# Row norms in a fused four-layer transformer kernel: the inverse root by one GpSimd power in place of eleven VectorE steps

## The reference, cut to what matters

```python
def _layernorm(x, axis=-1, eps=1e-05):
    m = jnp.mean(x, axis=axis, keepdims=True)
    v = jnp.var(x, axis=axis, keepdims=True)
    return (x - m) / jnp.sqrt(v + eps)

x = x + jnp.tanh(g_xattn[0]) * _L0_xattn_ref(_layernorm(x, axis=-1), ctx_1024, ctx_1024)
x = x + jnp.tanh(g_ffn[0]) * _L0_ffn_ref(_layernorm(x, axis=-1), ...)
x = x + jnp.tanh(g_xattn[1]) * _L1_xattn_ref(_layernorm(x, axis=-1), ctx_1024, ...)
x = x + jnp.tanh(g_ffn[1]) * _L1_ffn_ref(_layernorm(x, axis=-1), ...)
x = x + jnp.tanh(g_xattn[2]) * _L2_xattn_ref(_layernorm(x, axis=-1), ctx_1024, ctx_1024, mask_BxSxS2_bf0, ...)
x = x + jnp.tanh(g_ffn[2]) * _L2_ffn_ref(_layernorm(x, axis=-1), ...)
x = x + jnp.tanh(g_xattn[3]) * _L3_xattn_ref(ctx_1024, _layernorm(x, axis=-1), mask_BxS2_bf1, ...)
x = x + jnp.tanh(g_ffn[3]) * _L3_ffn_ref(_layernorm(x, axis=-1), ...)
```

## Time and profile before

| | |
|---|---|
| median of three runs | 1993.43 us |
| the profiled execution: its own time | 1995.64 us |
| its span, first to last instruction | 1993.9 us |
| PE busy | 1498.6 us, 75% |
| DVE busy | 1258.8 us, 63%, 4319 instructions |
| ACT busy | 782.1 us, 39% |
| POOL busy | 359.6 us, 18%, 242 instructions |
| mean granted clock of PE | 0.854 of full speed |

### The profile page before, as it was taken

One profiled execution on the slowest core, in us unless ns is written; L12 is line 12 of the kernel. 1 busy time (PEld: TensorE's weight loads), 2 busy tenths in 40 slices (PEclk: granted clock), 3 DMA queues, 4 the chain that ended last, 5 costly groups with the idle time before them and its releaser, 6 DMA issues. The chain is left out here.

```text
span 1993.9 us, 29626 instructions
## 1 busy us (share of the span) xinstructions
PE 1498.6 (75%) x10926; PEld 955.8 (48%) x10926; DVE 1258.8 (63%) x4319; ACT 782.1 (39%) x1473; POOL 359.6 (18%) x242
## 2 busy tenths in 40 slices
PE   5779586877688947787868875778786795778777
PEld 4447343553555724354545552346454464335545
DVE  5466875557646786555755688555564659755567
ACT  0335333653133523464314442356322353236522
POOL 0204101420031401240003230123002132014200
PEclk7889778988898968898779996889897897789988
DMA  7000000000000000000000000000000000000000
GB/s 286 1 1 1 0 1 0 1 1 14 7 1 1 1 0 1 1 1 13 2 7 1 1 1 1 1 1 2 14 1 7 1 1 1 1 1 1 1 14 6
DMA packets 16846, 19.80 MB, mean 10 GB/s; under 512 B 3352, under 2 KB 15400, under 8 KB 16172
## 3 DMA queue, kind: packets, MB, share of 16 engines
q1 hardware_dynamic: 16688, 17.75, 2.6%
HBM read 16.70 MB, written 1.05 MB: 9 GB/s over the span
## 5 line engine op out<-in xcount | busy, mean ns | idle before, releaser
L1003 POOL TENSOR_TENSOR work<-work 128x1024 f32<-128x1024 f32 x32 | 76.2, 2383 | 312.8 <-ACT work L987 312.8
L932 PE MATMUL bank<-xnT,w_f 128*128 128x512 f32 x256 | 123.2, 626 | 11.9 <-ACT work L984 11.9
L984 ACT ACTIVATE work<-bank,w_f 128x512 f32<-128x512 f32 x128 | 84.2, 684 | 108.9 <-PE bank L932 107.9
L943 PEld LDWEIGHTS bank<-w_f1d,work 128*128 128x128 f32 x1024 | 116.9, 192 | 7.7 <-ACT work L984 3.8
L943 PE MATMUL bank<-w_f1d,work 128*128 128x129 f32 x1024 | 116.9, 275 | 0.0
L1493 POOL TENSOR_TENSOR small<-small 128x16 f32<-128x16 f32 x28 | 81.3, 2903 | 191.1 <-DVE small L1514 190.9
L1513 DVE TENSOR_REDUCE small<-work 128x16 f32<-128x1024 f32 x48 | 58.3, 1215 | 90.4 <-ACT work L1404 86.4
L462 PE MATMUL bank<-consts,work 128*128 128x128 f32 x384 | 74.3, 331 | 50.0 <-ACT work L514 49.1
L1285 PE MATMUL bank<-consts,work 128*128 128x128 f32 x640 | 87.9, 283 | 27.7 <-ACT work L1413 10.7
L328 ACT COPY xnT<-bank 128x256 f32<-128x256 f32 x56 | 20.5, 373 | 211.0 <-PE bank L322 210.8
L462 PEld LDWEIGHTS bank<-consts,work 128*128 128x128 f32 x384 | 49.5, 165 | 108.9 <-ACT work L514 89.8
(11 more groups left out here) (278 smaller groups left out, 3490.5 us busy)
## 6 DMA issues: line engine op xcount, KB each, us to landing
w_f<-in_f_dram SPq DMA_DIRECT2D x1, 2616.0 KB
w_f<-in_f_dram SPq DMA_DIRECT2D x1, 2180.0 KB, 26.2
w_x<-in_x_dram SPq DMA_DIRECT2D x1, 2115.0 KB
w_l<-in_l_dram SPq DMA_DIRECT2D x1, 2088.5 KB, 21.2
w_f1d<-in_f1d_dram SPq DMA_DIRECT2D x4, 512.0 KB
work<-in_x_dram SPq DMA_DIRECT2D x5, 256.0 KB, 3.0
work<-in_ctx_dram SPq DMA_DIRECT2D x5, 256.0 KB, 3.4
out_dram<-x SPq DMA_DIRECT2D x4, 256.0 KB, 2.3
```

What stands on the lines that cost most here:

```text
L932: pe.matmul(banks[n % 3][:, :], k_f1["w1"][:, e * 512 + c * P:e * 512 + (c + 1) * P], xnT[:, :], start=True, stop=True).then_inc(up_done, 1)
L943: pe.matmul(z_of(e, t)[:, 0:129], hT[e % 2][:, c, t * P:(t + 1) * P], w_f1d[:, c, e, :], start=(c == 0), stop=(c == 3))
L984: act.activation(hT[e % 2][:, c, :], banks[n % 3][:, :], ACT.Relu, bias=k_f1["b1"][:, n:n + 1]).then_inc(hT_ready, 1)
L1003: link(pool.tensor_tensor(sq[e % 2][:, 0:2, :], sq[e % 2][:, 0:2, :], sq[e % 2][:, 2:4, :], ALU.add))
```

## The change

Where `norm_pair` stood behind the attentions of turns 1 and 3 and behind the perceiver, `norm_pair_by_pool` stands now, and `rms_pair`, behind the attention of turn 6, works in the same way: DVE writes variance plus epsilon of the pair's two tiles into a tensor of two columns and raises a semaphore, POOL takes both columns to the power -0.5 by one instruction, and DVE waits for it and goes on to the two scalings. `attention` gets a part for POOL (two such powers), the perceiver's part for POOL gets one behind `root_keys(6)` and one behind `root_keys(7)`. A column pair of -0.5 is set once ahead of the loop. `ffn0`, `ffn1`, `ffn2`, the opening of the next block and the last norm keep the eleven steps. `layer_norm` by POOL has fewer steps (`yield`s), so that `some(next_rows, 7)` in step 4 of `attention` now runs the whole norm of a pair, its wait for POOL and its scalings too. The core of the diff:

```diff
+        def ask_root(dve, ins):
+            ins.then_inc(variance_ready, 1)
+            roots["asked"] += 1
+            return roots["asked"]
+
+        def give_root(pool):
+            roots["given"] += 1
+            pool.wait_ge(variance_ready, roots["given"])
+            pool.tensor_tensor(root[:, :], variance[:, :], minus_half[:, :], ALU.pow).then_inc(root_ready, 1)
...
+            if by_pool:
+                rs = root
+                k = ask_root(dve, dve.tensor_scalar(variance[:, :], mv[:, :, 1], LN_EPS, None, ALU.add))
+                yield
+                dve.wait_ge(root_ready, k)
+            else:
+                link(dve.tensor_scalar(ve, mv[:, :, 1], LN_EPS, None, ALU.add))
+                yield
+                yield from rsqrt(dve, link, rs, ve, tmp)
...
+        def norm_pair_by_pool(dve, link, pair):
+
+            yield from layer_norm(dve, link, [(x, xn, t) for t in pair_tiles(pair)], by_pool=True)
+            dve.sem_inc(rows_ready, 1)
...
+        def rms_pair(dve, link, pair):
+
+            ms = scratch()[:, 0:2]
...
-            link(dve.tensor_scalar(ms, ms, 1.0 / D, RMS_EPS, ALU.mult, ALU.add))
+            k = ask_root(dve, dve.tensor_scalar(variance[:, :], ms, 1.0 / D, RMS_EPS, ALU.mult, ALU.add))
             yield
-            yield from rsqrt(dve, link, rs, ms, tmp)
-            return rs
...
+            dve.wait_ge(root_ready, k)
+            link.last_of([dve.scalar_tensor_tensor(xn[:, t, :], xn[:, t, :], root[:, t % 2:t % 2 + 1], k_f3["n1"],
                                                    ALU.mult, ALU.mult) for t in pair_tiles(pair)])
             dve.sem_inc(rows_ready, 1)
...
+                @block.gpsimd
+                def _(pool):
+                    for pair in range(2):
+                        give_root(pool)
...
+                        if b in (6, n - 1):
+                            give_root(pool)
...
+                pool.memset(minus_half[:, :], -0.5)
```

More of the change, by code:

```diff
@@ L184, in build @@
         small = sb("small", [P, 976])
+        variance = sb("variance", [P, 2])
+        root = sb("root", [P, 2])
+        minus_half = sb("minus_half", [P, 2])
         norm_small = sb("norm_small", [P, 256])
@@ L220, in build @@
         stages = []
-        flow = named("rows_ready rows_turned rowsT_ready dve_steps")
-        rows_ready, rows_turned, rowsT_ready, steps_sem = flow
+        flow = named("rows_ready rows_turned rowsT_ready dve_steps variance_ready root_ready")
+        rows_ready, rows_turned, rowsT_ready, steps_sem, variance_ready, root_ready = flow
         dve_steps = Chain(steps_sem)
@@ L238, in build, with layer_norm @@
         scratch.turn = 0
-        def layer_norm(dve, link, jobs):
+        roots = dict(asked=0, given=0)
+        def ask_root(dve, ins):
[6 more added lines that the diff above has]
+            pool.tensor_tensor(root[:, :], variance[:, :], minus_half[:, :], ALU.pow).then_inc(root_ready, 1)
+        def layer_norm(dve, link, jobs, by_pool=False):
             n, s = len(jobs), scratch()
@@ L249, in layer_norm @@
             yield
-            link(dve.tensor_scalar(ve, mv[:, :, 1], LN_EPS, None, ALU.add))
-            yield
-            yield from rsqrt(dve, link, rs, ve, tmp)
+            if by_pool:
[7 more added lines that the diff above has]
+                yield from rsqrt(dve, link, rs, ve, tmp)
             link.last_of([dve.tensor_scalar(dst[:, t, :], src[:, t, :], mv[:, k, 0:1], rs[:, k:k + 1],
@@ L268, in norm_pair_twice @@
             dve.sem_inc(rows_ready, 1)
-        def rms_scales(dve, link, pair):
-            s = scratch()
-            ms, rs, tmp = s[:, 0:2], s[:, 2:4], s[:, 4:6]
+        def rms_pair(dve, link, pair):
+            ms = scratch()[:, 0:2]
             link.last_of([dve.scalar_tensor_tensor(norm_rows[:, t % 2, :], xn[:, t, :], 1.0, xn[:, t, :], ALU.mult,
@@ L277, in rms_scales @@
             yield
-            link(dve.tensor_scalar(ms, ms, 1.0 / D, RMS_EPS, ALU.mult, ALU.add))
+            k = ask_root(dve, dve.tensor_scalar(variance[:, :], ms, 1.0 / D, RMS_EPS, ALU.mult, ALU.add))
             yield
-            yield from rsqrt(dve, link, rs, ms, tmp)
-            return rs
-        def rms_pair(dve, link, pair):
-            rs = yield from rms_scales(dve, link, pair)
-            link.last_of([dve.scalar_tensor_tensor(xn[:, t, :], xn[:, t, :], rs[:, t % 2:t % 2 + 1], k_f3["n1"],
+            dve.wait_ge(root_ready, k)
+            link.last_of([dve.scalar_tensor_tensor(xn[:, t, :], xn[:, t, :], root[:, t % 2:t % 2 + 1], k_f3["n1"],
                                                    ALU.mult, ALU.mult) for t in pair_tiles(pair)])
@@ L1861, in build @@
             prev = ffn0(i, None, 0, norm_pair)
-            prev = attention(prev, 1, norm_pair, k_x1, kv1, [], scaled[:, 0:1], None,
+            prev = attention(prev, 1, norm_pair_by_pool, k_x1, kv1, [], scaled[:, 0:1], None,
                              add_gated(lambda t: tg[:, 1:2], bo1[:, :]))
             prev = ffn1(prev, 2, norm_all)
-            prev = attention(prev, 3, norm_pair, k_x2, kv2, [(kv2.k_ready, 1), (kv2.v_ready, TILES)], None, neg2,
+            prev = attention(prev, 3, norm_pair_by_pool, k_x2, kv2, [(kv2.k_ready, 1), (kv2.v_ready, TILES)], None, neg2,
                              add_gated(lambda t: any2[:, t:t + 1]))
             prev = ffn2(prev, 4, norm_pair_twice)
-            prev = perceiver(prev, 5, norm_pair)
+            prev = perceiver(prev, 5, norm_pair_by_pool)
             prev = attention(prev, 6, rms_pair, k_a3, kv3, None, scaled[:, 1:2], None, add_to_z)
```

## The result

The change took 24 us off, not 9: the median is 1970.4 us (1961.41 to 1980.6) against 1994.51 us (1988.8 to 2002.07) for the kernel before, timed beside it; the ratio is 0.9876, with a 95% interval of 0.9844 to 0.9908. The profiled execution took 1973.64 us, with a span of 1970.8. The forecast was 1984.4 us and its range began at 1974, so the time lies outside it, on the fast side.

What follows compares the result with a forecast made beforehand. No engine is full; a chain of waits bounds the kernel, with 16.0 us of idle PE at the touched hand-overs. The terms -1.3 - 3.85 - 3.8 = -9 us took the median 1993.43 to 1984.4 us, range 1974 to 1999.

Steps and rivals of the forecast that it cites:

- What bounds the kernel: DVE's and PE's chains race for pair 1's transposes; PE idles 16.0 us at the 16 touched hand-overs.
- The round trip: DVE to POOL and back, a: semaphores 0.2 us plus 0.5 for a two-column power, so a = 0.7 us.
- The rival at a = 0.3: A cheaper power at the touched norms: 14 us gained, 1979.5 us; chance 0.15.
- the turn at 1.35: Round-trip length at which gain turns to loss, two columns taking 1.15 us; with the clock case, chance 0.18.
- The delay d: In the three attentions tile 3's reciprocal (L559) starts later: 0.64 us in turns 1 and 3, 0.44 in turn 6.
- Turns 1 and 3: Eight attention ends where PE's chain holds: 8 x 0.64 of delay less 6.4 us of idle, -1.3 us.
- Perceiver: Four ends without delay, each gaining the smaller of 1.5 us and PE's idle: 3.85 us.
- Turn 6: Four attention ends: 2.8 us gained in the first block, 1.0 in the other three, together -3.8 us.
- The rest at nothing: Everything outside the touched hand-overs, such as POOL's queue, the memset and removed DVE instructions, was counted as zero.
- PE's chain moves by d: In the attentions, projection, fill and both pairs' transposes follow L559 and shift by its delay, 0.64 or 0.44 us.
- The clock rival: Longer idle ahead of L488 flips fills to 1.2 GHz, 2.6 us each: 1993 us; chance 0.18 with a partly fixed power cost.
- The full gain of 1969.5: Nothing covers the gain: the full 1.5 us at all 16 ends, needing an earlier fill; chance 0.05.

Runs made afterwards that it cites:

- The late wait: Kernel after the change, with four or five empty steps between DVE's asking and its wait, so tile 3's reciprocal goes first: 1951.16 us, ratio 0.9757.
- the two families: Kernels before and after the change, each plain and with four or eight chained idle DVE steps per block; shift taken off: 1994.5, 1998.9, 1992.3 against 1970.4, 1966.5, 1971.6 us.
- the fill experiment: Kernel before the change, with two unread 512-column products on PE between the pairs' transposes in turns 2, 4, 6 and 7: 2000.13 us, ratio 1.0024.
- the kernel before with the shifts: Kernel before the change, with four or eight chained DVE steps that change nothing, once a block in ffn0: 2002.13 and 1998.66 us, ratios 1.0038 and 1.0031.
- the shifted pairs: Kernels before and after the change, both with four or both with eight chained idle DVE steps per block: 2002.13 against 1969.65 us, 1998.66 against 1978.04 us.
- the 14 kernels: The kernel before the change, the kernel after it and the twelve other kernels of the follow-up experiments, with ratios to the kernel before from 0.9583 to 1.0088.

## Why the prediction was wrong

**What bounds the kernel: right.** Idle of 16.0 us at the touched hand-overs, of which 0.4 us are left (0.25 and 0.13). The chains raced as described.

**The round trip: nearly right.** Forecast a = 0.7; DVE's idle is 0.81 us, as the power takes 0.70 (forecast 0.5) and the two semaphores 0.11. With 0.70, 1.01 and 2.90 us for 2, 4 and 16 columns, one column costs 0.157 us and 0.38 are fixed. The rule that two columns follow from the additions' fixed 0.16 gave 0.5; a power has more of its own. The rival at a = 0.3 is out, and so is the turn at 1.35. The Trainium skill's advice to keep elementwise work on VectorE (GPSIMD Engine Reference, Engine selection) compares one operation with one operation, and here 0.81 us stand against a chain of eleven, 2.18: no run contradicts the page, but taken for the chain it would have pointed the wrong way.

**The delay d: right as a delay.** The reciprocal starts 0.74 us later, forecast 0.64; PE's idle ahead of tile 3's projection is 2.66 us in the second block's turn 1, where it was 1.94, and 2.42 against 1.88 in turn 6. (In the first and third block's turn 1 it is 1.84 and 1.82, as PE's work ahead of it ended later there.) The late wait, which not only takes the delay away but lets the reciprocal start 0.54 us sooner than before, fits a delay that is paid in the total: 12 x 1.28 = 15 of its 19 us.

**With the measured a, the sum is still small.** Turns 1 and 3: 8 x 0.75 - 6.4 = -0.4. Perceiver: the gain of a second pair is 1.4, so -3.7. Turn 6: -2.6 in the first block and 3 x 0.55 - 2.3 = -0.6 in the others, -3.2. In all -7 us against -24 measured. The mis-sized a is not the error; it would have made the forecast worse.

**The largest step that failed: "The rest at nothing".** It held the stages behind at zero. By the stage times of the two profiled executions of the change itself, ffn1 and ffn3 give 5.0 and 4.1 us (5.8 and 4.4 in the two families), by the stretch at 1.2 GHz behind the hand-over, which ends with the idle. The control in the third block of ffn1 and the fill experiment's 57.45 against 55.4 us in ffn3 show the same within one kernel. That is 9.1 of the 16 us by which the spans' difference, 23.1 us, passes the 7.

**The second: "PE's chain moves by d".** It took all that stands ahead of L559 as unchanged but for the norm's steps, and all that PE does behind L488 as of fixed length. Behind it, from L488 to the end of the hand-over's copies, turns 1, 3 and 6 took 8.02, 7.37 and 7.46 us before, in every block, as DVE set it there; after, it is 7.08, 5.82 and 5.95 in the mean. The idle time that went from there was 1.01, 0.60 and 1.41 us in the mean. So turns 1 and 6 lost what fixed lengths allow, to within 0.1 us, and only turn 3 lost 0.95 us a block more, 4 us in all: its first block had 276.12 to 281.83 = 5.71 us from L488 to pair 0's transposes, and after it is 280.67 to 285.04 = 4.37, since the fill runs partly at 2.4 GHz now, 3.94 us for the same six pieces. Ahead of L559, the first parts, from the hand-over to tile 3's reciprocal, should have grown by d, in the sum 0.75 us in turns 1 and 3 and 0.55 in turn 6. They went from 23.65 to 23.36 us in turn 1, from 28.10 to 29.82 in turn 3 (which ate what its tail gave; hence its +0.2 in the table) and from 29.39 to 28.56 in turn 6.

**The idle time itself was read from one execution.** In the kernel before with the shifts, PE idled 10.8 us at turn 6's four hand-overs, in each of the two, and not 5.6. The same sum with the idle times of all three profiles gives -12 us instead of -7: turn 1 -1.6, turn 3 +0.6, perceiver -4.7, turn 6 -6.4. With the 10.2 us of ffn1 and ffn3 that is 22 of the 29 us in the table.

**The clock rival: right in what moves, wrong in direction.** It had the level of the fills as a free throw, which a longer idle ahead of L488 makes worse. The idle ahead of L488 did grow, and the fills did change level in more than two blocks (the text's own sign of being wrong), but both ways: behind turn 3 their mean fell from 5.08 to 4.46 us, behind turn 6 it grew from 4.41 to 4.59 (and from 3.31 to 4.71 in the shifted pairs). Over the whole page a piece went from 861 to 831 ns. The clock went up in all because of stretches that the prediction had no term for, those at the head of the next stage. It priced PE's idle as time lost once, and took the clock into the fills alone. The same sum by the clock itself: 38 us fewer at 1.2 GHz, each doing half the work of one at 2.4, is 19 us in the two profiled executions, and 11 by the medians, if PE set the pace throughout, which it doesn't (ffn2).

The Trainium skill (TensorE: Matmul & The Clock Gate, Part 1) advises not to fit a given number of cold products, the ramp being under 1% of a typical span. It speaks of a ramp; here 584 us of 1994 were at 1.2 GHz in 73 stretches, and taking some of them away at ffn1 and ffn3 gave 10 us, 0.5%. So as a size it agrees; as advice it hides here more than the whole forecast of 9 us.

**Range and chances.** The full gain of 1969.5 was the rival that came out, at 0.05, but by another way than it assumed: the fill didn't start earlier, and the 1.5 us weren't had at all 16 ends; stages that the sum held fixed got shorter. That its number fits is luck. "Lucky phase" for the change would have been an excuse, and the shifts speak against it.

**Left open.** Why the first parts did not grow by d. The clock inside them goes with it: their time at 1.2 GHz fell from 7.7 to 4.9 us in turn 1 and from 7.7 to 5.6 in turn 6, and rose from 12.0 to 15.1 in turn 3. Within the 14 kernels, block against block, turns 1 and 6 take 0.21 and 0.25 us more for each us of it (correlation 0.90 and 0.86; in turn 3 0.11 us and 0.46), which makes up a third to a half of the deviation from d in each turn. No run separated it, so it isn't shown to be the cause. The perceiver's 7.2 us stand against 4.7 that the idle at its hand-overs gives by the sum with all three profiles; in the two profiled executions of the change itself it is 3.6 against 3.7. In the full fill ffn1 takes 101.35 us and not the 100.94 of the kernel after; it had 29 us at 1.2 GHz there against 27.3, so it lost time to the clock elsewhere in the stage, and why wasn't tried.

## What to carry to other kernels

Price an idle gap of PE at a hand-over twice: once as its length, and again as the stretch at half clock that may follow it in a stage nobody touched (1.7 us behind a gap of 0.74 here, nothing in ffn2, where PE doesn't set the pace). Read the gap from several executions, since it was 16 us in one of the kernel before and 22 and 26 in its shifted forms. A chain of tiny dependent steps on one engine is worth moving to an idle engine that does it in one instruction, if the round trip is short against the chain; then put the next independent work between asking and waiting, which here gave 19 us more on top of 24. Before believing such a gain, shift the whole program by fractions of a microsecond, before and after: if the two families don't overlap, a lucky phase is an unlikely cause.

## What the runs showed of the hardware

A GpSimd power costs 0.70 us for 2 columns, 1.01 for 4 and 2.90 for 16: 0.38 us are fixed and 0.157 come with each column. It is short enough to stand in a critical chain. The round trip from DVE to POOL and back adds only 0.11 us to it (0.81 of DVE's idle), or 0.12 with 16 columns (3.02). At the hand-overs into ffn1, ffn2 and ffn3, TensorE's clock fell to 1.2 GHz within 3 us behind the transposes only where PE had been idle for 0.15 us or more ahead of them, 47 of 78 times with idle and 0 of 90 without. A stretch of 3.41 us at 1.2 GHz cost ffn1 1.7 us, and cost ffn2 nothing that its stage time shows.
